# A graph-attention layer on one core: the softmax's drops summed on VectorE instead of by a product, and the one-hots of a place stored once per node

## What is computed

```
hs = (x @ Ws + bs).reshape(N, H, HD)
hd = (x @ Wd + bd).reshape(N, H, HD)
e = leaky_relu(hs[src] + hd[dst], 0.2)
logits = einsum('ehd,hd->eh', e, attn)
m = segment_max(logits, dst)
ex = exp(logits - m[dst]);  s = segment_sum(ex, dst)
out = segment_sum((ex / s[dst])[..., None] * hs[src], dst)
```

## Time and profile before

| | |
|---|---|
| time, median of 3 runs | 2149.63 us (2147.95 to 2150.61) |
| the profiled execution's own time | 2149.37 us |
| its span, first to last instruction | 2147.3 us |
| mean granted TensorE clock | 0.984 of 2.4 GHz |
| busy, share of the span | PE 96%, VectorE 77%, ScalarE 54%, GpSimd 45% |

### The profile page before, as it was taken

One profiled execution on the slowest core, in us unless ns is written; L12 is line 12 of the kernel. 1 busy time (PEld: TensorE's weight loads), 2 busy tenths in 40 slices (PEclk: granted clock), 3 DMA queues, 4 the chain that ended last, 5 costly groups with the idle time before them and its releaser, 6 DMA issues. The chain is left out here.

```text
span 2147.3 us, 85544 instructions
## 1 busy us (share of the span) xinstructions
PE 2057.0 (96%) x29551; PEld 1669.1 (78%) x29552; DVE 1652.7 (77%) x3737; ACT 1160.0 (54%) x3113; POOL 975.0 (45%) x1023
## 2 busy tenths in 40 slices
PE   7999999998899999999998899899999999999798
PEld 4665555555799999999997555589999999999676
DVE  5545882564699999999998764489999999999884
ACT  2101200014677777777775423477777777777584
POOL 0000010120577777777773211267777777777020
PEclk9999999999999999999999999999999999999899
DMA  6000233995788888888884224488888888888411
GB/s 202 1 0 8 82 106 122 261 277 148 226 269 270 264 276 271 270 267 277 270 271 140 90 88 135 126 252 271 271 270 269 272 262 279 272 267 271 182 58 50
DMA packets 191648, 427.41 MB, mean 199 GB/s; under 512 B 60291, under 2 KB 128841, under 8 KB 191537
## 3 DMA queue, kind: packets, MB, share of 16 engines
q0 software_dynamic: 59584, 298.64, 44.8%
q1 hardware_dynamic: 128155, 119.85, 18.3%
q10 hardware_dynamic: 3828, 7.85, 1.1%
HBM read 385.68 MB, written 29.10 MB: 193 GB/s over the span
## 5 line engine op out<-in xcount | busy, mean ns | idle before, releaser
L531 ACT ACTIVATE at_relu<-at_turned,ah_attn_size 128x512 f32<-128x512 f32 x1092 | 713.4, 687 | 308.5 <-PE at_turned L605 298.2
L507 POOL DMA_INDIRECT at_rows<-table,ah_index x360 | 425.0, 1180 | 176.2 <-POOL ah_index L495 72.0
L507 POOL DMA_INDIRECT ah_room<-table,ah_index x352 | 422.1, 1199 | 167.9 <-POOL ah_index L495 65.8
L711 DVE SCALAR_TENSOR_TENSOR at_relu<-at_relu,ah_pair_sign 128x512 f32<-128x512 f32 x546 | 377.1, 744 | 9.4 <-ACT at_relu L531 9.3
L741 DVE SCALAR_TENSOR_TENSOR sums<-sums,at_factor,at_total 128x97 f32 x1456 | 358.5, 307 | 4.5 <-PE at_total L647 1.1
L601 PE MATMUL at_turned<-ident,ah_room 128*128 128x128 f32 x2208 | 341.7, 278 | 19.0 <-PEq L1701 19.0
L601 PE MATMUL at_turned<-ident,at_rows 128*128 128x128 f32 x2160 | 331.0, 276 | 0.1
L601 PEld LDWEIGHTS at_turned<-ident,ah_room 128*128 128x128 f32 x2208 | 243.9, 142 | 39.9 <-issue 39.8
L601 PEld LDWEIGHTS at_turned<-ident,at_rows 128*128 128x128 f32 x2160 | 236.3, 141 | 19.9 <-issue 19.9
L731 DVE TENSOR_TENSOR at_spread<-at_lined,at_weight 128x1024 f32<-128x1024 bf16 x182 | 221.4, 1217 | 4.1 <-ACT at_weight L542 4.1
L605 PE MATMUL at_turned<-ah_place,dst_rows 96*128 96x128 bf16 x2208 | 216.0, 220 | 0.0
(11 more groups left out here) (315 smaller groups left out, 2904.2 us busy)
## 6 DMA issues: line engine op xcount, KB each, us to landing
at_flags<-run_flags SPq DMA_DIRECT2D x182, 64.0 KB
dst_rows<-pr_parts SPq DMA_DIRECT2D x76, 144.0 KB, 2.7
ah_place<-places SPq DMA_DIRECT2D x92, 96.0 KB
dst_rows<-local_rows SPq DMA_DIRECT2D x13, 672.0 KB, 4.9
places<-dst_rows SPq DMA_DIRECT2D x13, 672.0 KB, 6.8
at_place<-places SPq DMA_DIRECT2D x90, 96.0 KB
table<-ah_room SPq DMA_DIRECT2D x20, 400.0 KB, 4.9
ah_room<-table,ah_index POOLq DMA_INDIRECT x368
```

The source lines that it names most:

```text
L507: pool.indirect_dma_start(rows[b][:, j, :], None, table, bass.IndirectOffsetOnAxis(index[b][:, j:j + 1], 0)).then_inc(gathered[b], 16)
L531: act.activation(relu[c][:], turned[chunk(b, c)][:], ACT.Relu, scale=attn_size[:, c:c + 1]).then_inc(bent, 1)
L711: dve.scalar_tensor_tensor(relu[c][:], relu[from_][:], pair_sign[:, c:c + 1], relu[c][:], ALU.mult, ALU.add).then_inc(joined, 1)
```

## The change

Two parts. **The drops.** ScalarE's `drops` multiplies the rise with the whole `head_rows` (128x128; the result is written over `iota_row`, which is not needed any more). PE turns this with one transposing pass (`turn_drops`) in place of the product. VectorE sums groups of four columns of it out of PSUM into a small tile, `fold` (`fold_drops`), in the round in which the macro is `message`, between the third join and the first adds. ScalarE's `factors` reads `fold` and waits for it (`folded`).

**The one-hots.** `places` holds 32 rows for a macro and no longer 96; whoever loads it lets a row land on three partitions. The building takes up to 28 macros at a time on all 128 partitions, in four builds (28, 28, 28 and 7 macros), between source tiles 1 to 8. ScalarE's queue issues their loads and stores, and SP's does none of it.

```diff
-        places=dram("places", [NM, SP_ROWS, ME], BF16),
+        places=dram("places", [NM, S, ME], BF16),
...
-        drop = sb("at_drop", [P, G * HH])
+        drop, fold = iota_row, sb("at_fold", [P, G, HH])
...
-                    sp.dma_start(place[b][:], places[bass.ds(m, 1)].rearrange("o p e -> (o p) e")).then_inc(local_loaded[b], 16)
+                    sp.dma_start(place[b][:], places[bass.ds(m, 1)].rearrange("o n e -> (o n) e").unsqueeze(1).broadcast_to([S, SPLIT, ME])).then_inc(local_loaded[b], 16)
...
-                    act.activation(drop[:], quarter_mask[:, 0], ACT.Relu, scale=rise[:]).then_inc(dropped, 1)
+                    act.activation(drop[:], head_rows[:], ACT.Relu, scale=rise[:]).then_inc(dropped, 1)
...
                 def factors(m, b):
-                    act.wait_ge(turned_back, 2 * m + 2)
+                    act.wait_ge(folded, m + 1)
                     for j in range(G):
-                        act.activation(factor[b % 2][:, j, :], back[:, P + j * HH:P + (j + 1) * HH], ACT.Exp,
+                        act.activation(factor[b % 2][:, j, :], fold[:, j, :], ACT.Exp,
                                        scale=first_dst[:, bass.ds(m * G + j, 1)]).then_inc(weights_ready, 1)
...
-                def sum_drops(m):
+                def turn_drops(m):
...
-                    pe.matmul(back[:, P:P + G * HH], head_rows[:], drop[:], start=True, stop=True).then_inc(turned_back, 1)
+                    pe.transpose(back[:, P:2 * P], drop[:], ident[:]).then_inc(turned_back, 1)
...
+                def fold_drops(m):
+                    dve.wait_ge(turned_back, 2 * m + 2)
+                    dve.tensor_reduce(fold[:], back[:, P:2 * P].rearrange("p (j k g) -> p j k g", j=G, g=HM)[:, :, 0:HH, :], AX.X, ALU.add).then_inc(folded, 1)
+
...
                     if head:
                         for k in range(len(JOINED)):
                             join(head[0], k)
+                    if message:
+                        fold_drops(message[0])
                     if message:
                         for j in range(1):
                             add_total(message[0], message[1], j, at)
...
+                    act.dma_start(many[k % 2][0:groups * S], local_rows[at:at + groups * BATCH].rearrange("(q m) j e -> q (m j e)", q=groups)
+                                  .unsqueeze(1).broadcast_to([groups, S, BATCH * ME])).then_inc(many_loaded[k % 2], 16)
...
+                    for k in range(len(BUILDS)):
+                        store_many(k)
+                        if k + 2 < len(BUILDS):
+                            load_many(k + 2)
+                        store_ruled(k)
...
                     for t in range(NT):
                         source(t)
-                        build(t)
+                        if t in BUILD_SLOTS:
+                            build(BUILD_SLOTS.index(t))
+                        if t - 1 in BUILD_SLOTS:
+                            rule(BUILD_SLOTS.index(t - 1))
```

More of the change, by code:

```diff
@@ L680, in slot @@
                     if head:
[L681 removed]
+                        turn_drops(head[0])
                     if turn:
@@ L1640 @@
 MOVED_FIRST = sum(TURN_PARTS[1])
-BATCH = 7
-BATCHES, BUILT = NM // BATCH, 5
-assert BATCH * BATCHES == NM and NT < BATCHES <= NT + 3 and BATCH * ME <= (NT - BUILT) * D
+BATCH, BUILT = 7, 5
+BUILDS = [(at, min(QS, (NM - at) // BATCH)) for at in range(0, NM, QS * BATCH)]
+BUILD_SLOTS = range(1, 2 * len(BUILDS), 2)
+assert NM % BATCH == 0 and BUILD_SLOTS[-1] + 1 < NT and QS * BATCH * S * G <= (NT - BUILT) * D and BATCH * ME <= (NT - BUILT) * D
 assert sum(n for _, n in TURN_PARTS) == NT
@@ L1654, in heads_half, with turnover @@
     return ap.rearrange("p (g x) -> p g x", x=H * QUAD)[:, :, half * H * QUAD // 2:(half + 1) * H * QUAD // 2]
-def turnover(layer, ahead, Wsrc, bsrc, Wdst, bdst, attn, ln_w, ln_b, sums, dst_rows, worn, index_ready, local_loaded, gathered, nc, ident, iota_row, split_of, local_rows, dst_local, places, lines, nodes, table, head_mask,
+def turnover(layer, ahead, Wsrc, bsrc, Wdst, bdst, attn, ln_w, ln_b, sums, dst_rows, worn, index_ready, local_loaded, gathered, nc, ident, iota_row, node_of, local_rows, dst_local, places, lines, nodes, table, head_mask,
              src_index, run_flags, global_rows, **_):
@@ L1786, in _ @@
                     load_w(w_dst, Wdst, dst_w_loaded)
-                    load_many(0)
-                    load_many(1)
                     for t in range(NT):
                         store(t)
-                        store_many(t)
-                        load_many(t + 2)
-                    sp.wait_ge(many_stored[0], 16)
+                    for b in range(2):
+                        sp.wait_ge(many_stored[b], 16 * sum(groups for _, groups in BUILDS[b::2]))
                 sp.wait_ge(fresh, 1)
                 for b in range(2):
-                    sp.dma_start(ahead.place[b][:], places[b]).then_inc(local_loaded[b], 16)
+                    sp.dma_start(ahead.place[b][:], places[b].unsqueeze(1).broadcast_to([S, SPLIT, ME])).then_inc(local_loaded[b], 16)
                 for t in range(NT):
@@ L1959, in build, with rule @@
                 def build(k):
+                    at, groups = BUILDS[k]
                     dve.wait_ge(many_loaded[k % 2], 16 * (k // 2 + 1))
-                    dve.tensor_scalar(many[k % 2], many[k % 2], split_of[0:SP_ROWS], None, ALU.is_equal).then_inc(many_made, 1)
+                    here = many[k % 2][0:groups * S]
+                    dve.tensor_scalar(here, here, node_of[0:groups * S], None, ALU.is_equal).then_inc(many_made, 1)
+                def rule(k):
+                    at, groups = BUILDS[k]
                     if k > 1:
                         dve.wait_ge(ruled_stored[k % 2], 16 * (k // 2))
-                    dve.tensor_tensor(ruled[k % 2], over(iota_row[:, 0:S], BATCH * G),
-                                      dst_local[:, k * BATCH:(k + 1) * BATCH, :].rearrange("p m j -> p (m j)").unsqueeze(2).broadcast_to([P, BATCH * G, S]),
+                    lists = groups * BATCH * G
+                    dve.tensor_tensor(ruled[k % 2][:, 0:lists], over(iota_row[:, 0:S], lists),
+                                      dst_local[:, at:at + groups * BATCH, :].rearrange("p m j -> p (m j)").unsqueeze(2).broadcast_to([P, lists, S]),
                                       ALU.is_equal).then_inc(ruled_made, 1)
```

53 lines of the change are left out of this document (24 added, 29 removed).

## The result

The changed kernel takes **2398.55 us** (median; 2397.3, 2398.0 and 2399.1 in the runs compared) against 2149.91 us of the kernel before on the same chip: a ratio of **1.116**, interval 1.1142 to 1.1179. It is slower by 249 us. One more execution of the changed kernel took 4390.36 us at a granted clock of 0.51 over the whole of it and is left out of the comparison: none of the twelve executions of three further kernels with the same pauses of PE (the wait alone, and the two with one more reduce) shows this, so that its cause, and whether the pauses had a part in it, stays open. The profiled execution took 2397.3 us, its span is 2395.6 us.

A forecast was written before the change was run, and what follows sets the result against it. PE was taken to bound the rounds, with VectorE close behind. 2149.4 + 234 (wait in the rounds) + 1 (layers' ends) - 4 (one-hots) = 2380 us; 8-in-10 range 2335 to 2435.

The forecast's parts named there:

- The likeliest case: Rounds of both layers: a closed chain from scan to scan takes 8.10 us against 6.80, +234 us; chance 0.87.
- scan to the end of the third join: VectorE's own work in a round, without idle time and not shortened by the change: 5.74 us.
- the fold, beyond the join's end: VectorE's new reduce out of PSUM behind the third join, sized between two neighbouring instructions: 0.20 us.
- factors' start to bend 5's end: ScalarE's four factors and the bend queued behind them, read from the earlier timeline: 1.31 us.
- bend 5's end to the next scan: PE's last two products up to VectorE's scan, read from the start of the layer: 0.75 us.
- The margin of bend 5: Before the change, ScalarE ends bend 5 ahead of its need by the second product of PE's `sum_heads`: 0.16 us.
- the wait never shows: Rival: factors find the fold done or bend 5 stays in time, PE goes on bounding: 2127 to 2145 us; chance 0.05.
- The ends of the layers: Last macro of each layer: the last fold stands behind VectorE's other work and adds wait, some 0.5 us a layer, +1 us.
- The one-hots: First turnover: PE's 4.12 us wait behind VectorE and a late load goes, -4 us, bounds -6 to +4.
- The pass for the product, the wide drop: Rounds: PE's shorter pass counted as nothing; ScalarE's drop takes 0.1 us more, covered by the third join.
- the case at 3330 us: Rival: PE's pauses in the rounds drop its clock to 1.2 GHz, layers 1190 us longer; chance 0.03.
- What the profile would show: Gap 8.1 us; ScalarE and PE idle about 1.3, VectorE over 1 ahead of the scan; fold 0.2; clock 1.00.

The follow-up runs named there:

- the wait alone: Changed kernel with the earlier product and small drop; VectorE only copies 8 numbers into `fold` behind the third join, and `factors` waits for that: 2390.99 us, ratio 1.1144.
- the two with one more reduce: Changed kernel with an extra VectorE reduce of 128 numbers for nobody: just ahead of the fold 2432.69 us, behind the first two adds 2397.84 us.
- the copy: Changed kernel with the earlier product and small drop; VectorE copies 8 numbers ahead of the joins in place of the fold, factors read SBUF: 2154.76 us, ratio 1.0033.
- the one-hots alone: Changed kernel with drops, product and factors out of PSUM as before and no fold; only the new `places` and builds stay: 2142.35 us, ratio 0.9985.

## Why the prediction was right, point by point

The likeliest case came true: slower, 2398.55 us in a range of 2335 to 2435, by the chain that was named. Its links, as measured in the round shown, 809.74 to 817.98:

| link | predicted | measured |
|---|---|---|
| scan to the end of the third join | 5.74 | 815.48 - 809.74 = 5.74 |
| the fold, beyond the join's end | 0.20 | 815.58 - 815.48 = 0.10 |
| hand-over to ScalarE | 0.10 | 815.70 - 815.58 = 0.12 |
| factors' start to bend 5's end | 1.31 | 817.13 - 815.70 = 1.43 |
| bend 5's end to the next scan | 0.75 | 817.98 - 817.13 = 0.85 |
| round | 8.10 | 8.24 (mean 8.20) |

The sum was 18 us low in 180 gaps, and three links were off. One of them has the other sign, so that a part of the closeness is luck: without it the sum would have been 36 us low.
- **The fold** is 0.18 us long, as sized between its neighbours, but it starts 0.08 before the join ends. I had seen this overlap on ScalarE and not used it on VectorE: -0.10.
- **Factors to bend 5**, +0.12: the sum took their length out of PSUM. Read out of SBUF the four take 0.85, waiting or not (the copy and the fold ahead of the joins show it without a wait). The prediction had the edit, "now reading SBUF", only among the reasons for a shorter time; it made it longer.
- **Bend 5 to scan**, +0.10: I took the layer's first round, where the scan starts 0.07 us behind the products' end. In the round shown it is 0.18, and the earlier trace rows had it: 805.82 - (804.80 + 0.84). Over the rounds of the changed kernel it is 0.07 in some and 0.17 in others, so that the mean is off by half of that, and the mean round is 8.20. PE's start behind bend 5 was right (0.05).

**The margin of bend 5** was misread. The three products were put at 0.28 us each, a third of 0.84, but the second starts 0.22 behind the first (0.84 - 0.62): bend 5 was 0.10 us early and not 0.16, the third join 0.45 and not 0.6. The sum of 8.10 does not use this, as the chain goes from the end of bend 5. The case in which the wait never shows does: its 2127 to 2145 us leave out what the change adds on ScalarE. With the fold ahead of the joins there is no such wait, and the time is 2171.8 us; only with the products in another order, 2138.83, does it come into that range.

**The ends of the layers** were put at +1 us together. The last adds stand 8.04 us behind the last scan of layer one where they stood 6.96, and 8.05 in place of 7.25 in layer two: 1.1 and 0.8 us. Of the first almost nothing is left when the second layer's rounds start (+0.2 in all between them); of the second, 2.3 us are there at the end of the span, 1.5 of which lie in the tail and were not followed.

**The one-hots**: -4 us predicted, -6.0 in the profiled execution (0.15%, some 3 us, by the ratio of the one-hots alone). The changed kernel's PE and VectorE in the turnover:

```profile
452.01 77.67 PE L1892 MATMUL pr_ps<-pr_w_dst,sums 128*128 128x384 f32 x240
```

```profile
400.08 1.15 DVE L1976 TENSOR_SCALAR dst_rows<-dst_rows,node_of 128x3584 bf16<-128x3584 bf16 x1 [7.31 <-DMA dst_rows<-local_rows]
...
406.28 3.89 DVE L1983 TENSOR_TENSOR dst_rows<-iota_row,dst_local 128x3584 bf16<-128x3584 f32 x1
```

The pause is gone: 240 products in 77.67 us without a break, where the second half alone took 40.66 behind its pause of 4.12. That half was also 1.7 us longer than the first; the first half, and the granted clock behind the pause, in the kernel before:

```profile
451.78 38.97 PE L1879 MATMUL pr_ps<-pr_w_dst,sums 128*128 128x384 f32 x120
```

```profile
495.00:500.00 5.00, 5.00 (x11) 2.79 (x12) 3.52 (x7) 3.31 (x7) 0.00 (x0) 0.66 0.98 250
```

In the 5 us behind the pause the granted clock was 0.66, so the pause cost 4.12 us of standing and some 1.7 of slow products. The prediction counted the first alone; without the pause both are gone, some 5.8 of the 6.0. VectorE still waits 7.31 us for the first load, and PE's source pass goes on over it (79.33 us as before): the bound of +4 did not come.

**The pass for the product, the wide drop**: counted at nothing, and in the changed kernel they are (the wait alone comes to 1.1144). For the drop my reason, that 0.1 us ahead of bend 4 is covered by the join, holds only while ScalarE waits anyway; in a kernel without the wait it takes 0.1 where bend 5 has 0.05 to spare.

**The clock** stayed at 1.00 in the windows of both layers' rounds, with pauses of PE of 1.2 us in each of 8.2; behind the one pause of 4.12 us in the turnover before, it was 0.66. The Trainium skill, TensorE: Matmul & The Clock Gate, A second HAM failure mode: psum-queue depth-cycling, says that frequent short idle times between groups of products can make the clock swing; by the windows of the two layers it does not at pauses of 1.2 us, and the case at 3330 us did not come in the runs compared.

**The wait never shows** fell with the 214.3 us ahead of the factors. **What the profile would show** was right for the gap, ScalarE, PE, the fold and the clock. One place was wrong: VectorE's long idle time stands ahead of the adds (1.23 us, for the factors), and ahead of the scan it is 0.64, as I had reckoned that the adds lie inside VectorE's wait and not seen that the wait for them comes first in its queue.

## What to carry to other kernels

Before an input of an instruction is moved to another engine, write down what stands behind the reader in its in-order queue and what stands ahead of the new writer in its own. If something behind the one is needed for what the other does next, a loop closes, and what stands in it, one link behind the other, sets the round, not the load of an engine; here 0.18 us of work behind the joins cost 1.4 us a round, and ahead of them, with all else the same, 0.16. Then work out the margin of each engine that is not the bound (0.05 us here), from the start of the instruction that needs the result and with the hand-over: two edits that each cost next to nothing beside it may cost more than their sum together, and the order of the consumer's own steps may give it back.

## What the runs showed of the hardware that was not expected

- ScalarE takes longer over small tiles out of SBUF than out of PSUM: four 128x2 exponentials take 0.73 us out of PSUM and 0.85 out of SBUF, with the same destination and no wait in either. One alone takes about as long (medians 0.279 and 0.294 us); they start further apart, 0.74/4 = 0.185 us and not 0.58/4 = 0.145. The Trainium skill, ScalarE: Activation LUTs, Step-by-step: what each stage is for, says that ScalarE is closer to PSUM, of the tile that it writes; these rows agree in direction, for the tile that it reads.
- An instruction of VectorE may start before the end of the one ahead of it, also when it reads PSUM: the fold starts 0.08 us before the third join ends, and the reduce ahead of the fold delays it by 0.19 us though it is 0.28 long.
- A reduce of 32 numbers to 8 out of PSUM takes 0.183 us (median of 182), a copy of 8 numbers out of it 0.159.
